# Two-layer cross-attention on one core: third norm as rows, new order of the last attention tiles, W2 split earlier on GpSimd, 48 turns of the identity at the start

## The reference, cut to what matters

```python
# layer 0, x [16,128,256], y [16,128,192], 16 heads of 16
xn = layernorm(x, ln1_w, ln1_b);  yn = layernorm(y, ln2_w, ln2_b)
attn = softmax((xn @ Wq) @ k.T * scale);  k, v = split(yn @ Wkv)
x = x + (attn @ v) @ Wproj + bproj
x = x + gelu(layernorm(x, ln3_w, ln3_b) @ W1 + b1) @ W2 + b2    # the third norm; W1 256x1024, W2 1024x256
# layer 1: RMS norm, rotated and normalised q and k, softmax attention on the same y
x = x + (softmax(unit(q) @ unit(k).T * 4) @ v) @ wout
```

## Time and profile before

| | us |
|---|---|
| median of 3 runs | 406.68 (406.52 to 407.26) |
| the profiled execution, its own time | 405.8 |
| its span, first to last instruction | 403.9 |
| mean granted TensorE clock | 0.975 of full speed |

### The profile page before, as it was taken

How to read it: one execution, slowest core, us unless ns; L and a number is a source line. 1 busy time by engine, 2 the same in 40 slices (tenths; PEclk the granted TensorE clock), 3 DMA queues, 4 the chain that set the end, 5 groups by cost and what they waited for, 6 DMA issues and landing times.

```text
span 403.9 us, 11390 instructions
## 1 busy us (share of the span) xinstructions
PE 356.9 (88%) x4432; PEld 321.8 (80%) x4432; DVE 284.6 (70%) x640; ACT 238.8 (59%) x462; POOL 198.5 (49%) x177
## 2 busy tenths in 40 slices
PE   0678999999999998779999999989889898998984
PEld 0568888888888887669999999989778787887863
DVE  4785398898988967116555445555899999999853
ACT  1242357767677663383466545553788787887762
POOL 2453245344454538100433320508789989899820
PEclk9995799999999999899999999998999999999999
DMA  6943000110000000000000000000000010110001
GB/s 164 232 138 114 24 25 26 27 41 30 26 2 2 23 2 2 2 0 2 2 0 0 0 0 2 7 14 11 10 21 13 26 46 23 45 36 13 28 28 41
DMA packets 15256, 12.58 MB, mean 31 GB/s; under 512 B 3568, under 2 KB 14576, under 8 KB 15216
## 3 DMA queue, kind: packets, MB, share of 16 engines
q1 hardware_dynamic: 14144, 10.91, 9.3%
q10 hardware_dynamic: 1072, 1.11, 1.1%
HBM read 9.92 MB, written 2.10 MB: 30 GB/s over the span
## 4 chain that ended last, share of the span: by engine, by line
PE 57%; issue 22%; DVE 8%; POOL 6%; ACT 4%; DMA 2%; ACTq 0%; POOLq 0%; DVEq 0%
PE bank_qk L668 9%; PE banks_s L716 6%; PE bank_y L798 4%; PE bank_qk L693 4%; PE bank_qk L697 3%; PE banks_s L968 3%; PE bank_t L764 3%; PE bank_y L792 3%; PE bank_o L707 3%; PE bank_t L668 2%; DMA ln_rows<-in_L_xattn_ln_b 2%; PE bank_y L988 2%; DVE row_max L1137 2%; PE bank_y L660 2%; POOL x_all L358 2%
## 5 line engine op out<-in xcount | busy, mean ns | idle before, releaser
L394 POOL TENSOR_TENSOR norm_inv<-norm_sq_min,minus_half 128x32 f32<-128x32 f32 x16 | 87.4, 5466 | 1.8 <-DVE norm_sq_min L1301 1.8
L334 POOL TENSOR_TENSOR masked<-qkT_r,halves_t 128x512 fp32r<-128x512 f32 x32 | 32.8, 1047 | 39.6 <-DVE qkT_r L1127 39.6
L537 ACT ACTIVATE W_s<-banks_s,b_all 128x256 f32<-128x256 f32 x60 | 25.0, 468 | 39.3 <-PE banks_s L847 39.3
L1137 DVE TENSOR_REDUCE row_max<-banks_s 128x8 f32<-128x1024 f32 x32 | 37.6, 1218 | 9.3 <-PE banks_s L716 9.1
L461 ACT ACTIVATE PT<-banks_s 128x1024 f32<-128x1024 f32 x32 | 31.0, 1021 | 21.4 <-PE banks_s L747 21.4
L351 POOL TENSOR_TENSOR b_var_eps<-b_mean_var,eps_t 128x2 f32<-128x2 f32 x8 | 1.6, 197 | 73.1 <-DVE b_mean_var L1075 73.1
L847 PE MATMUL banks_s<-lnT_hi,W_hi 128*128 128x256 f32 x120 | 34.3, 286 | 0.0
L847 PE MATMUL banks_s<-lnT_lo,W_hi 128*128 128x256 f32 x120 | 33.9, 283 | 0.0
L847 PE MATMUL banks_s<-lnT_hi,W_lo 128*128 128x256 f32 x120 | 33.9, 283 | 0.0
L716 PE MATMUL banks_s<-masked,qkT_r 32*128 32x256 f32 x768 | 32.2, 298 | 1.8 <-DVE row_max L1137 1.5
L603 ACT ACTIVATE PT<-banks_s 128x1024 f32<-128x1024 f32 x32 | 31.1, 1025 | 4.1 <-PE banks_s L968 4.1
(11 more groups left out here) (154 smaller groups left out, 1097.5 us busy)
## 6 DMA issues: line engine op xcount, KB each, us to landing
ctx_in<-in_ctx SPq DMA_DIRECT2D x32, 96.0 KB, 2.0
x_all<-in_x SPq DMA_DIRECT2D x16, 128.0 KB, 2.1
W_s<-in_L_xattn_W SPq DMA_DIRECT2D x2, 1024.0 KB, 7.0
out<-Wq_s SPq DMA_DIRECT2D x16, 128.0 KB, 1.7
Wq_s<-in_L_xattn_Wq ACTq DMA_DIRECT2D x1, 256.0 KB, 6.9
Wkv_s<-in_L_xattn_Wkv ACTq DMA_DIRECT2D x1, 256.0 KB, 7.5
Wproj_s<-in_L_xattn_Wproj SPq DMA_DIRECT2D x1, 256.0 KB, 2.9
wout_s<-in_L_xattn_wout SPq DMA_DIRECT2D x1, 256.0 KB, 3.1
```

The costliest lines, as they stand in the source:

```text
L334: nc.gpsimd.tensor_tensor(masked[:, r, 1, :, half, :], qkT_r[:, r, 1, :, :].bitcast(fp32), ones, ALU.mult)\
L394: nc.gpsimd.tensor_tensor(norm_inv[:, j, :], norm_sq_min[:, j, :], minus_half[:, :], ALU.pow)\
L537: last = nc.scalar.activation(hT[:, m, :], bank_s[u][:, 256 * k:256 * k + 256], ACT.Gelu, bias=b1_all[:, m:m + 1])
L1137: v.tensor_reduce(row_max[:, 8 * h:8 * h + 8], banks_s[:, 2 * h:2 * h + 2, :].rearrange("p n (r k) -> p (n r) k", k=TOK), AX.X, ALU.max).t ...
```

## The change

Five edits:

1. The weight and bias of the third norm are loaded as rows over all partitions (`ln3_rows`, in the space of `rot_sq`, which only stage C uses). `normalise_b` has four `scalar_tensor_tensor` where two `tensor_scalar` were; the first two do not wait for the inverse deviation. W1 is split without a scale. `mlp_bias`, the addition to b1 and their waits go.
2. W2 is split in steps 8 to 15 on POOL, one instruction a step behind `masked_lo`, four copies, then four subtractions.
3. The last tiles: the maxima of tiles 14 and 15 are turned into bank_t and no longer into bank_qk, earlier in the order of the PE; parts 0 and 1 of `up_b(0)` follow later; part 1 goes from bank_qk straight into the GELU, without a raw copy. `weighted_a` of the last three tiles waits for the maxima to be copied out of bank_t. ACT's and DVE's orders are changed to match.
4. In every step the wait for the copied maxima stands behind the score terms of `shifted_a`, in front of the 16 small matmuls that read them.
5. 48 transposes of the identity into bank_s on the PE, between the wait for the identity and `inputs_a(0)`.

```diff
-            for n, w in enumerate((ln3_w, ln3_b, norm_w)):
-                sp.dma_start(ln_cols[:, n, :], w.rearrange("(t p) -> p t", p=128), ...)
+            for n, w in enumerate((ln3_w, ln3_b)):
+                sp.dma_start(ln3_rows[:, n, :], w.unsqueeze(0).broadcast_to([128, C1])).then_inc(w_b1_loaded, LOADED)
+            sp.dma_start(norm_cols[:, :], norm_w.rearrange("(t p) -> p t", p=128), ...)
...
@@ gpsimd, for s in range(2, NB + 1): step_a(s)
+                if s == 8:
+                    pool.wait_ge(w_mlp_loaded, 5 * LOADED)
+                if 8 <= s < 12:
+                    nc.gpsimd.tensor_copy(W2_hi[:, part(s - 8), :], W2_s[:, part(s - 8), :]).then_inc(w2_hi_done, 1)
+                if 12 <= s < NB:
+                    u = s - 12
+                    pool.wait_ge(w2_hi_done, u + 1)
+                    nc.gpsimd.tensor_tensor(W2_lo[:, part(u), :], W2_s[:, part(u), :], W2_hi[:, part(u), :].bitcast(fp32), ALU.subtract)
...
-            pool.wait_ge(w_mlp_loaded, 5 * LOADED)
             pool.wait_ge(b_bias, 2)
-            for u in range(4):
-                nc.gpsimd.tensor_copy(...)
-            pool.wait_ge(w2_hi_done, 4)
-            for u in range(4):
-                nc.gpsimd.tensor_tensor(...)
@@ scalar, behind step_a(NB)
             lnT_b(0, False)
             exps_a(NB - 3)
+            maxima_T(NB - 2, bank_t)
             on_T(NB - 4)
+            values_a(NB - 1)
             out_T(NB - 3)
-            values_a(NB - 1)
+            exps_a(NB - 2)
+            maxima_T(NB - 1, bank_t)
             raw_b(0)
-            maxima_T(NB - 2)
-            exps_a(NB - 2)
             on_T(NB - 3)
+            exps_a(NB - 1)
             out_T(NB - 2)
-            raw_b(1)
-            maxima_T(NB - 1)
...
-            exps_a(NB - 1)
+            act.wait_ge(w_b1_loaded, 4 * LOADED)
+            gelu_first(0)
             on_T(NB - 2)
+            gelu_b(0, False, [1], bank_qk)
             out_T(NB - 1)
-            act.wait_ge(w_mlp_ready, 1)
-            gelu_first(0)
-            gelu_first(1)
+            gelu_b(0, False, [2])
             on_T(NB - 1)
-            gelu_b(0, False, [2, 3])
+            gelu_b(0, False, [3])
@@ tensor
-            def mlp_bias():
-                ...
             def shifted_a(t):
-                    pe.wait_ge(a_maxT, t + 1)
                     pe.wait_ge(a_maxed, 2 * upto(t + 2))
                     wait(pe, A["exped"], 2 * t)
                     score_terms(t, KT, 0, False)
+                    pe.wait_ge(a_maxT, t + 1)
...
@@ weighted_a
                     if t > NB - 4:
                         pe.wait_ge(b_lnT_lo, 1)
+                        pe.wait_ge(a_maxT, t + 2 if t < NB - 1 else NB)
...
             pe.wait_ge(ident_ready, 2)
+            for n in range(WARM):
+                nc.tensor.transpose(bank_s[n % 4][:, 0:128], ident[:, :], ident[:, :])
             inputs_a(0)
...
-            mlp_bias()
             step_a(4)
-            pe.wait_ge(w_mlp_ready, 1)
...
             scores_a(NB - 1)
+            maxima_a(NB - 2, bank_t)
             weighted_a(NB - 3)
             project_a(NB - 4)
+            shifted_a(NB - 2)
+            maxima_a(NB - 1, bank_t)
             pe.wait_ge(w1_lo_done, 4)
-            pe.wait_ge(a_maxT, NB - 2)
+            pe.wait_ge(a_qk_lo, NB)
             up_b(0, False, [0], bank_qk)
-            pe.wait_ge(b_raw, 1)
-            maxima_a(NB - 2)
             back_a(NB - 3)
-            shifted_a(NB - 2)
             normed_a(NB - 3)
+            shifted_a(NB - 1)
             weighted_a(NB - 2)
             project_a(NB - 3)
-            pe.wait_ge(a_maxT, NB - 1)
+            pe.wait_ge(b_raw, 1)
             up_b(0, False, [1], bank_qk)
-            pe.wait_ge(b_raw, 2)
-            maxima_a(NB - 1)
             back_a(NB - 2)
-            shifted_a(NB - 1)
             normed_a(NB - 2)
             weighted_a(NB - 1)
+            up_b(0, False, [2])
             project_a(NB - 2)
-            up_b(0, False, [2])
             back_a(NB - 1)
@@ vector
-                scale = ln_cols[:, 0, u % 2:u % 2 + 1]
-                v.tensor_scalar(w1_part(W1_hi, u), w1_part(W1_s, u), scale, None, ALU.mult)
+                v.tensor_copy(w1_part(W1_hi, u), w1_part(W1_s, u))
-                v.scalar_tensor_tensor(w1_part(W1_lo, u), ..., ALU.mult, ALU.subtract)
+                v.tensor_tensor(w1_part(W1_lo, u), w1_part(W1_s, u), w1_part(W1_hi, u).bitcast(fp32), ALU.subtract)
             def normalise_b(p, later):
                 dve.wait_ge(b_stats, 2 * p + 2)
-                dve.wait_ge(b_rstd, p + 1)
                 if later:
                     dve.wait_ge(b_T, p)
                 for j in range(2):
-                    v.tensor_scalar(b_xn[:, j, :], tile_of(2 * p + j), mean, rstd, ALU.subtract, ALU.mult)
+                    v.scalar_tensor_tensor(b_xn[:, j, :], tile_of(2 * p + j), mean, ln3_rows[:, 0, :], ALU.subtract, ALU.mult)
+                dve.wait_ge(b_rstd, p + 1)
+                for j in range(2):
+                    dve.wait_ge(b_centred, 2 * p + j + 1)
+                    v.scalar_tensor_tensor(b_xn[:, j, :], b_xn[:, j, :], rstd, ln3_rows[:, 1, :], ALU.mult, ALU.add)
...
-            dve.wait_ge(b1_mm, 1)
-            v.tensor_tensor(b1_all[:, :], bank_y[:, 0:HM], b1_cols[:, :], ALU.add)
...
             step_a(NB)
+            split_lnT(0)
+            heads_a(NB - 4)
+            residual_a(NB - 5)
             dve.wait_ge(A["res_ready"], 4)
             stats_b(1)
-            heads_a(NB - 4)
-            residual_a(NB - 5)
-            split_lnT(0)
             maxima(NB - 1)
+            residual_a(NB - 4)
             heads_a(NB - 3)
-            residual_a(NB - 4)
             normalise_b(1, True)
+            residual_a(NB - 3)
             heads_a(NB - 2)
-            residual_a(NB - 3)
             residual_a(NB - 2)
```

More of the change, by code:

```diff
@@ L50 @@
 AHEAD = 4
+WARM = 48
 STEPS_C = NB + 7
@@ L150, in build @@
         onT_r = sb("onT_r", 128, 2, KT, TOK, dtype=fp32r)
-        ln_cols = sb("ln_cols", 128, 3, KT)
+        norm_cols = sb("norm_cols", 128, KT)
+        ln3_rows = rot_sq[:, :].rearrange("p (n c) -> p n c", n=2)
         b1_cols = sb("b1_cols", 128, HM)
-        b1_all = sb("b1_all", 128, HM)
         bproj_row = sb("bproj_row", 128, C1)
@@ L361, in _ @@
                 step_a(s)
+                if s == 8:
[5 more added lines that the diff above has]
+                    pool.wait_ge(w2_hi_done, u + 1)
+                    nc.gpsimd.tensor_tensor(W2_lo[:, part(u), :], W2_s[:, part(u), :], W2_hi[:, part(u), :].bitcast(fp32),
+                                            ALU.subtract).then_inc(w2_lo_done, 1)
                 if s == 12:
@@ L452, in maxima_T @@
                     wait(act, a_shifted, t)
-                    nc.scalar.activation(maxT[:, :], bank_qk[:, 0:TOK], ACT.Copy).then_inc(a_maxT, 1)
+                    nc.scalar.activation(maxT[:, :], bank[:, 0:TOK], ACT.Copy).then_inc(a_maxT, 1)
             def exps_a(t):
@@ L523, in gelu_first @@
                 for m in (2 * u, 2 * u + 1):
-                    last = nc.scalar.activation(hT[:, m, :], hT[:, m, :], ACT.Gelu, bias=b1_all[:, m:m + 1])
+                    last = nc.scalar.activation(hT[:, m, :], hT[:, m, :], ACT.Gelu, bias=b1_cols[:, m:m + 1])
                 last.then_inc(b_gelu, 1)
@@ L527, in gelu_first, with gelu_b @@
                 nc.scalar.activation(hT_hi[:, part(u), :], hT[:, part(u), :], ACT.Copy).then_inc(b_hT_hi, 1)
-            def gelu_b(p, later, parts=range(4)):
+            def gelu_b(p, later, parts=range(4), bank=None):
                 for u in parts:
@@ L536, in gelu_b @@
                         m = 2 * u + k
-                        last = nc.scalar.activation(hT[:, m, :], bank_s[u][:, 256 * k:256 * k + 256], ACT.Gelu,
-                                                    bias=b1_all[:, m:m + 1])
+                        last = nc.scalar.activation(hT[:, m, :], (bank or bank_s[u])[:, 256 * k:256 * k + 256], ACT.Gelu,
+                                                    bias=b1_cols[:, m:m + 1])
                     last.then_inc(b_gelu, 1)
@@ L653, in _ @@
             mm = nc.tensor.matmul
-            def mlp_bias():
-                pe.wait_ge(w1_loaded, LOADED)
-                pe.wait_ge(w_b1_loaded, 4 * LOADED)
-                for m in range(HM):
-                    for k in range(KT):
-                        last = mm(bank_y[:, m:m + 1], W1_s[:, k, 128 * m:128 * m + 128], ln_cols[:, 1, k:k + 1],
-                                  start=k == 0, stop=k == KT - 1)
-                last.then_inc(b1_mm, 1)
             def split_mm(out, a, b):
@@ L1247, in _ @@
             for k in range(KT):
-                scale = ln_cols[:, 2, k:k + 1]
+                scale = norm_cols[:, k:k + 1]
                 hi, lo, w = by_tile(wq_r[:, 0, k, :]), by_tile(wq_r[:, 1, k, :]), by_quad(wq_s[:, k, :])
```

38 lines of the change are left out of this document (20 added, 18 removed).

## The result

The changed kernel takes 395.28 us (median of 4 runs, 394.17 to 397.70) against 406.66 us (4 runs, 406.52 to 407.26): 0.9726 of the time before, 95% interval 0.9678 to 0.9773. That is 11.4 us less, where 13.7 were forecast. The four runs lie 3.5 us apart, those of the kernel before 0.7; but 34 further executions of the kernel before, taken beside the experiments, spread over 3.3 us (9 at 405.35 to 405.88, 22 at 406.56 to 407.48, 3 at 408.61 to 408.67), so a wide spread is not new with the change, and the profiled execution of before, at 405.8, lies in the lowest of these three groups.

What follows compares the result with a forecast made beforehand. PE time and PE waits were taken as the bound; -6.85 - 1.2 - 2.0 + 0 + 0.4 - 4.05 = -13.7 gave 393.0 us against 406.68, own range 391 to 394.5, with rivals (1) to (3) 390.3 to 397.0.

Steps and rivals of the forecast that it cites:

- rival (1): At the start, the turns win nothing because the clock drops again in the wait before tile 0: 395.0 us, chance 0.24.
- The products for b1: Ahead of tile 3's queries, removing these PE products saves their whole 6.85 us, since no engine works in their cover.
- The clock in tile 3's step: After the removed products, the clock is back near 36 us, so less is lost to half clock: -1.2 us.
- The turns: At the start, 48 identity transposes are hidden and bring tile 0's loads to full speed: -2.0 us.
- W2's split: Moved on POOL into steps 8 to 15, it costs 0 us, bounds 0 and 1.6.
- rival (3): POOL's split blocks DVE in steps 12 to 15 and DVE's order delays `inputs_a`: +1.4, 394.4 us, chance 0.08.
- The norm: The third norm's four DVE operations instead of two, in step 14 and stage B: +0.4 us, bounds +0.2 and +2.0.
- The weave: Where stages A and B interleave, the new order of the last tiles and a steadier clock save 4.05 us.
- the second fall: Half clock in the weave from 165.5 to 168.3 us, costing 1.4 us; its absence was a named sign.
- Rival (2): The weave stays late, ACT becomes its bound and the clock falls again; half of 4.05 remains: 395.0 us, chance 0.14.
- (4): From 32 us on the clock stays at half for 13.3 us: +3.45 instead of -1.2, 397.7 us, chance 0.07.
- (5): Slower than before: the clock stays low into the PE-bound steps, 409.7 us with two such steps, chance 0.03.

Runs made afterwards that it cites:

- b1_products: The changed kernel with the 32 one-column products for b1 put back between steps 3 and 4, their result unused: 402.64 us.
- again: The changed kernel itself repeated with nothing edited, the yardstick also called the repetition: 396.20 us.
- late_turns: The changed kernel with its 48 turns plus 13 and 10 turns of the identity in the PE's two waits of step 3: 393.02 us.
- w2_late: The changed kernel with POOL's eight operations of W2's split back after stage A, as before the change: 395.70 us.
- no_warm: The changed kernel without the 48 turns of the identity at the start: 397.01 us.
- late_bias: The changed kernel with POOL's addition of the output bias waiting until DVE has made the low halves of h of the previous pair: 395.49 us.
- old_tail: The changed kernel with the last attention tiles in the old order on PE, ACT and DVE: 399.96 us.

## Why the prediction was right, and where it was not

The forecast was 393.0 us, 390.3 to 397.0; measured 395.28. It is the stated range that held, because it took in rivals (1) to (3); the forecast's own, 391 to 394.5, missed, and 395.28 is the time of rival (1), 395.0 at a chance of 0.24. The large terms held, the two on the clock and the one on the norm did not, and all three of these erred on the side of too much gain.

**The products for b1 (-6.85): right.** 7.0 us between the traces, 6.9 in the pair `b1_products` and `again`, 6.4 at the medians. Nothing took their place.

**The clock in tile 3's step (-1.2): failed.** I expected full speed near 36 us, from the fall in the weave, which I took to last 2.8 us. (Its windows of 0.53 and 0.76 make it 165.1 to 168.5, 3.4 us, since a window of 0.76 between the levels 0.50 and 1.00 is at half for 0.48 of it; in the same way the half clock of before ran to 45.6 and not 45.3. Neither correction would have saved the term.) In after it fell at 33.3 and came back at about 40.1 us, 6.8 us, and tile 3's step gained 0.1. The result lies between the bounds: the long stretch of half clock was in part that of the one-column products (with them it ran to 45 us, `b1_products`), in part not. I took the row that was nearest in kind of work, from another place. Filled, the step gives 2.1 us, and 1.0 more comes in the scores ahead of it (`late_turns`).

**The turns (-2.0): failed as the likeliest case, and rival (1) was the one that occurred.** The half-speed loads of the earlier trace rows were read correctly, and the 48 turns were hidden, ending at 9.16. What failed is "the idleness is about 2 us and the clock elsewhere survived gaps of that size in part": in the trace of after it did not survive at 12 us, nor at 19. In one execution (`w2_late`) it did at 12. Both outcomes occur with the same instructions up to there, and the forecast took the better one for the rule. Alone the turns gained 0.6 to 1.4 us, which these runs cannot tell from nothing; with the waits behind them filled, 4.0. The Trainium skill says that the PE's clock is throttled by default and rises with activity ("TensorE: Matmul & The Clock Gate", Part 1); the traces agree, and add that at these waits of 2 us it falls in some executions and not in others.

The start of this trace of after is 1.2 us later than before rather than 2.0 earlier: the fall at 19 us is absent from the one trace of before. The turns are not the cause, as `no_warm` without them comes to the same place at 25.8. Whether the fall is absent in all executions of before is open, and their spread of 3.3 us makes it doubtful, as the one with a trace, at 405.8 us, lies in the lowest group. So this row of the table is no sure measure of what the change did to the start.

**W2's split (0): right within 0.5 us.** The eight operations cost nothing in steps 8 to 15 that a median shows, and rival (3), +1.4, did not come. POOL and DVE did meet: in step 15 a cast of 16 columns took 1.06 us beside `W_lo`, hidden behind PE's work:

```profile
136.33 1.28 POOL L371 TENSOR_TENSOR W_lo<-W_s,W_hi 128x512 fp32r<-128x512 f32 x1
...
136.58 1.06 DVE L1140 CAST max_cols<-row_max 128x16 fp32r<-128x16 f32 x1
```

Out of the weave it saved 0.45 us, which the forecast had as 0.

**The norm (+0.4): mis-sized, 1.9 us, at its upper bound of 2.0.** Step 14 lost 0.3, within the term, though at 8.64 us it passed the 8.5 that I had named as a sign of being wrong. Stage B lost 1.5 instead of 0.3. I counted the length of the norm where the PE waits for it, and not who would be let through behind it: with the norm of four operations DVE's low halves of `h` are held up by POOL's addition of the bias, where with two it was POOL, and the PE waits for them (at 187.00 in after). That is 1.3 us by `late_bias`. Why the direction turned is not shown, since POOL starts 0.28 us behind DVE either way. The rule of the Trainium skill ("SBUF — State Buffer", on the shared port pair) that the forecast weighed for W2 in steps 12 to 15 was the right rule for another place; `hT_lo` and the `x_all` addition both read two SBUF inputs, and the trace agrees with it: 3.57 us for four low halves against 2.49. The remaining 0.4 us of the 1.9 in the table are there with the old norm as well (78.53 against 78.12), and have no cause that I have shown.

**The weave (-4.05): right, 4.2 us.** Of it 1.4 us are the clock, as priced, and 2.8 the order, where 3.15 less 0.5 for handoffs were forecast; `down_b(0)` came at 172.84 for the 169 forecast, late by the errors ahead of it (3.2 at the start, 1.1 in the clock) and not by its own. Its exponentials stand beside the raw products as worked out, and the second fall is gone in after and present in `old_tail`. Rival (2) did not come.

**Rivals (4) and (5)** did not occur: the stretch of half clock at 33 us lasted 6.8 us, where (4) had 13.3 and my own sign of being right was 4 or less.

The sum with the sizes measured is -6.9 + 0 (clock) - 1.2 (turns) - 0.4 (W2) + 1.9 + 0.4 (stage B, unexplained) - 3.8 (order, by `old_tail`) = -10.0; the medians give -10.6 (repetition) to -11.4. The two profiled executions give only -8.0, because that of before lies 0.9 us under its median and that of after 2.4 over.

## What to carry to other kernels

In this kernel a PE wait of 1.4 to 2.3 us ahead of a burst cost more than its own length when the clock fell behind it: 1.5 us on top in stage C, 3.1 in step 3. Warming the PE before the first burst paid clearly only once the next waits were bridged too: with all of them filled by turns that nothing reads, some 6 us more were won (396.2 to 388.7, less 1.3 for POOL's bias), and the spread between runs went from 4 us to under 2. When an edit changes an operation on DVE, look at which pair of DVE and POOL instructions with two SBUF inputs stands side by side behind it, and let a semaphore hold back the engine whose work nobody awaits. Delete PE work that no other engine can cover first: here that term came out as counted.

## What the runs showed of the hardware, not expected

- The granted clock is a matter of the execution: with the same instructions up to there it stayed at 1.00 (`w2_late`) or fell to 0.50 (after) at 13 us, and the wait of 2.3 us ahead of stage C's tile 2 has a fall in eight traces of thirteen.
- The granted column reads 1.00 ahead of its first change, though loads run at half speed there: eight loads took 1.78 us at a shown 1.00, 0.97 at full speed.
- Thirty-two products of one column, issued back to back for 6.99 us, left the clock at 0.50, where it had fallen before them; it rose in ordinary products behind them, at 45.6 us in `b1_products` and in before. No run has them begin at 1.00.
- The sizes of the collision of DVE and POOL, and that its direction turned with POOL starting 0.28 us behind DVE both times. DVE's subtraction of 16 columns takes 0.18 us alone and 1.21 beside POOL's 128x512; POOL's two additions take 1.45 us alone and 3.50 beside DVE's low halves.
- What stays open: the worth of the 48 turns by themselves (about 1 us, within the spread), why the collision turned, whether before's start is usually that of its trace, and the 0.4 us of stage B.
